# Row loads ahead of the small copies, two weight pieces shared between GpSimd and VectorE, and a new order around the group borders

## The reference

```python
q, k = rope(x @ Wq.T), rope(x @ Wk.T)            # bf16, one head of 256
o    = where(causal, exp(q @ k.T / 16), 0).sum(-1)   # one number per token
x1   = layernorm(x + relu(o * fc1_w + fc1_b) @ fc2_w.T + fc2_b)
xa   = x1 @ P_w.T                                # 64 values
C1, C2, C3 = top-3-of-12 softmax of xa @ U1.T, xa @ U2.T, xa @ U3.T
h    = gelu(sum_e C1[:, e] * (x1 @ W1[e].T))
y    = layernorm(x1 + sum_e C2[:, e] * (h @ W2[e].T) + C3 @ b2)
```

## Time and profile before

| | us |
|---|---|
| median of 3 runs | 297.56 |
| the profiled execution's own time | 297.77 |
| its span | 296.0 |
| busy TensorE / VectorE / GpSimd / ScalarE | 262.5 / 215.9 / 181.3 / 175.9 |

### The profile page before, as it was taken

How to read it: one execution, slowest core, us unless ns; L and a number is a source line. 1 busy time by engine, 2 the same in 40 slices (tenths; PEclk the granted TensorE clock), 3 DMA queues, 4 the chain that set the end, 5 groups by cost and what they waited for, 6 DMA issues and landing times.

```text
span 296.0 us, 6482 instructions
## 1 busy us (share of the span) xinstructions
PE 262.5 (89%) x2016; PEld 193.3 (65%) x2016; DVE 215.9 (73%) x668; ACT 175.9 (59%) x376; POOL 181.3 (61%) x367
## 2 busy tenths in 40 slices
PE   8999939999979597889799899898998998989960
PEld 5444414454536376767589798797897896878950
DVE  0369626969984965989599899899897877764660
ACT  2246932666565153655766967967878859464531
POOL 2630001897998999755676576785785765755532
PEclk9999995999999889999799999999999999999995
DMA  8997499998000000000000010101010010110101
GB/s 226 405 392 267 77 175 163 206 137 103 0 0 3 0 0 3 0 6 15 21 13 26 21 37 20 38 19 40 18 29 27 20 38 18 40 36 21 36 23 54
DMA packets 19546, 20.51 MB, mean 69 GB/s; under 512 B 1643, under 2 KB 18870, under 8 KB 18998
## 3 DMA queue, kind: packets, MB, share of 16 engines
q1 hardware_dynamic: 18518, 19.14, 28.2%
q10 hardware_dynamic: 992, 0.93, 1.1%
HBM read 15.78 MB, written 4.19 MB: 67 GB/s over the span
## 4 chain that ended last, share of the span: by engine, by line
PE 48%; POOL 15%; SPq 11%; DVE 11%; issue 6%; ACT 5%; DMA 2%; POOLq 0%; DVEq 0%; ACTq 0%
PE bank L1108 35%; PE bank L916 5%; POOL W L470 5%; POOL wtmp L467 4%; DVE early L1521 4%; POOL W L469 3%; SPq L393 2%; SPq L380 2%; DMA xs<-in_x 2%; PE bank L991 2%; SPq L371 2%; PE bank L1186 2%; SPq L398 2%; ACT early L726 1%; SPq L397 1%
## 5 line engine op out<-in xcount | busy, mean ns | idle before, releaser
L1108 PE MATMUL bank<-W,x1T 128*128 (+1 forms) x630 | 77.3, 278 | 6.0 <-DVE early L1521 3.1
L1108 PE MATMUL bank<-W,early 128*128 (+1 forms) x630 | 74.4, 273 | 3.0 <-DVE early L1561 1.3
L1108 PEld LDWEIGHTS bank<-W,x1T 128*128 128x128 f16 x630 | 61.7, 100 | 17.1 <-issue 5.5
L1108 PEld LDWEIGHTS bank<-W,early 128*128 128x128 f16 x630 | 61.0, 98 | 10.8 <-DVE early L1561 1.6
L916 PE MATMUL bank<-early,wqk 128*128 128x512 f32 x128 | 62.1, 617 | 0.2 <-DMA early<-in_xT 0.2
L1521 DVE SCALAR_TENSOR_TENSOR early<-bank,Csel,early 128x256 f32<-128x256 f32 x95 | 45.7, 481 | 15.7 <-PE bank L1108 6.7
L590 POOL TENSOR_TENSOR early<-early 128x256 f32<-128x256 f32 x29 | 21.1, 729 | 31.6 <-DVE early L1521 31.6
L661 ACT ACTIVATE qk<-bank 128x512 bf16<-128x512 f32 x32 | 19.0, 595 | 32.3 <-PE bank L916 32.2
L916 PEld LDWEIGHTS bank<-early,wqk 128*128 128x128 f32 x128 | 22.9, 195 | 21.0 <-issue 20.3
L787 ACT ACTIVATE early<-early 128x256 f32<-128x256 f32 x32 | 13.3, 417 | 36.5 <-DVE early L1521 36.4
L1274 DVE TENSOR_TENSOR xturn<-qk,turn 128x2048 bf16<-128x2048 bf16 x16 | 21.2, 1323 | 16.1 <-ACT qk L661 16.1
(11 more groups left out here) (139 smaller groups left out, 460.7 us busy)
## 6 DMA issues: line engine op xcount, KB each, us to landing
early<-in_xT SPq DMA_DIRECT2D x16, 256.0 KB, 8.5
xs<-in_x SPq DMA_DIRECT2D x32, 128.0 KB, 7.9
out<-early SPq DMA_DIRECT2D x32, 128.0 KB
W<-in_w1T SPq DMA_DIRECT2D x1, 2048.0 KB, 12.2
W<-in_w2T SPq DMA_DIRECT2D x1, 2048.0 KB, 12.9
W<-in_w1T SPq DMA_DIRECT2D x1, 1024.0 KB, 7.6
W<-in_w2T SPq DMA_DIRECT2D x1, 1024.0 KB, 14.6
wqk<-in_wqkT ACTq DMA_DIRECT2D x1, 512.0 KB, 3.7
```

Of the source, the lines that this page charges most:

```text
L1108: mm = pe.matmul(where[:, 0:DIM], lhs(hx, c), w, start=(k == 0), stop=(k == 5))
```

## The change

Six things change.

1. SyncE issues `load_rows(0)`, chunks 4 and 5 and `load_rows(1)` before the twelve copies.
2. Of the last two pieces of W2 (numbers 14 and 15; `SHARED` is 14) GpSimd makes only the high half, in one multiply from `Wf` to `W`. VectorE makes the low half (`piece_rest`). Piece 15 may only be written when VectorE has read piece 14's source.
3. GpSimd does `chosen_exps(0)` and `weights_of(0)` one piece earlier, and `bias_add(0, 0)` between the last two pieces.
4. TensorE's `route_count(0)` comes behind the third projection of chunk 7. Tile 0's second mixture takes the experts in the order 0 to 11, with other waits.
5. At the borders of groups 1, 6 and 7 TensorE does the first mixture of the group's first tile between the two bias halves; ScalarE's `final(1)` moves behind a `bias_copy`.
6. At the end VectorE does the statistics of tile 30 before the second mixture of tile 31.

```diff
@@ sync
-            sp.wait_ge(fc2_split, 1)
-            sp.wait_ge(b2_split, 1)
-            for k in range(NP):
-                sp.dma_start(fc2s[NI * k:NI * (k + 1), :], fc2p[:, RIGHT[k], :]).then_inc(fc2_spread, 16)
-                sp.dma_start(b2s[NE * k:NE * (k + 1), :], b2p[:, RIGHT[k], :]).then_inc(b2_spread, 16)
             load_rows(0)
             for c in range(4, NCH):
                 load_chunk(c)
                 if c % 2:
                     load_rows(c // 2 - 1)
+                if c == 5:
+                    sp.wait_ge(fc2_split, 1)
+                    sp.wait_ge(b2_split, 1)
+                    for k in range(NP):
+                        sp.dma_start(fc2s[...], fc2p[:, RIGHT[k], :]).then_inc(fc2_spread, 16)
+                        sp.dma_start(b2s[...], b2p[:, RIGHT[k], :]).then_inc(b2_spread, 16)
@@ gpsimd, w_piece (SHARED = NM * (NE - NB) - 2)
+                if n >= SHARED:
+                    if n == SHARED:
+                        pool.wait_ge(w_split, SHARED)
+                    else:
+                        pool.wait_ge(piece_low, n - SHARED)
+                    pool.tensor_scalar(W[:, m, e + 1, 0, :], Wf[:, WS * m + e + 2, :], scale[:, 1 + m:2 + m], 0.0,
+                                       ALU.mult, ALU.add).then_inc(piece_high, 1)
+                    return
@@ gpsimd
-                    if (c, j) == (6, 2):
+                    if (c, j) == (6, 1):
                         chosen_exps(0)
                         weights_of(0)
...
+            bias_add(0, 0)
             w_piece(piece)
...
-            bias_add(0, 0)
             norm_scale(2)
@@ scalar, aux
                 if (k, s, pos) == (1, 0, 0):
                     normed(3, 0)
-                    final(1)
                 if (s, pos) == (0, 1):
                     if group(k):
                         bias_copy(k, 0)
+                    if k == 1:
+                        final(1)
@@ tensor
+            def between(k):
+                return k in (1, NG - 2, NG - 1)
...
                     if group(k):
                         bias(k, 0)
+                    if between(k):
+                        routed_first(GT * k)
                     if later(k + 2):
                         x1_transpose(k + 2, 0)
...
+                if c == NCH - 1:
+                    route_count(0)
                 if c:
                     scores(c - 1, 1)
...
             route_logits(1)
+            pe.wait_ge(wlo_done, NM * NB)
+            second(0, range(0, NB))
             pe.wait_ge(w_split, NM * (NE - NB) - 2)
-            second(0, range(0, 6))
+            second(0, range(NB, NB + 2))
             bias(0, 1)
+            second(0, range(NB + 2, NE - 2))
             x1_transpose(2, 0)
-            pe.wait_ge(w_split, NM * (NE - NB))
-            second(0, range(6, NE - NB))
-            pe.wait_ge(wlo_done, NM * NB)
-            second(0, range(NE - NB, NE))
+            pe.wait_ge(piece_low, 2)
+            second(0, range(NE - 2, NE))
@@ vector
+            def piece_rest(n):
+                e = NB + n % (NE - NB)
+                dve.wait_ge(piece_high, n - SHARED + 1)
+                dve.scalar_tensor_tensor(W[:, 1, e + 1, 1, :], Wf[:, WS + e + 2, :], scale[:, 2:3], W[:, 1, e + 1, 0, :],
+                                         ALU.mult, ALU.subtract).then_inc(piece_low, 1)
...
             first_mixture(0, range(8, NE))
+            piece_rest(SHARED)
             norm_stats(2)
             h_low(0)
+            piece_rest(SHARED + 1)
             first_mixture(1)
...
                 aux(k, s, 0)
+                if i == NT + 1:
+                    row_stats(i - 3)
                 second_mixture(i - 2)
-                if late(i - 3):
+                if late(i - 3) and i <= NT:
                     row_stats(i - 3)
```

More of the change, by code:

```diff
@@ L199, in build @@
         KEPT = 10
+        SHARED = NM * (NE - NB) - 2
         ld_qk = sem("ld_qk")
@@ L232, in build @@
         wlo_done = sem("wlo_done")
+        piece_high = sem("piece_high")
+        piece_low = sem("piece_low")
         proj_done = sem("proj_done")
@@ L327, in build @@
         before = [max((k for k in range(n) if place[k] == place[n]), default=None) for n in range(len(taker))]
-        def dense_expert(m, j):
-            return (j + NB * m) % NE
         def last(t, m):
@@ L403, in _ @@
                     load_rows(c // 2 - 1)
+                if c == 5:
+                    sp.wait_ge(fc2_split, 1)
+                    sp.wait_ge(b2_split, 1)
+                    for k in range(NP):
+                        sp.dma_start(fc2s[NI * k:NI * (k + 1), :], fc2p[:, RIGHT[k], :]).then_inc(fc2_spread, 16)
+                        sp.dma_start(b2s[NE * k:NE * (k + 1), :], b2p[:, RIGHT[k], :]).then_inc(b2_spread, 16)
             load_rows(TPS - 1)
@@ L1069, in early @@
                     fc(k + 3, 0)
-                if (s, pos) == (3, 1) and group(k + 1):
-                    route_count(k + 1)
             def aux(k, s, pos):
@@ L1117, in mixture @@
                         pe.wait_ge(acc_begun if act else slot_added, count)
-                    e = dense_expert(m, j) + 1 if t == 0 else held_ids[t // GT][REC * m + j]
+                    e = j + 1 if t == 0 else held_ids[t // GT][REC * m + j]
                     products(bank[place[n]], lhs, m, e).then_inc(slot_done, 1)
@@ L1203, in _ @@
             route_logits(1)
+            pe.wait_ge(wlo_done, NM * NB)
+            second(0, range(0, NB))
             pe.wait_ge(w_split, NM * (NE - NB) - 2)
-            second(0, range(0, 6))
+            second(0, range(NB, NB + 2))
             bias(0, 1)
+            second(0, range(NB + 2, NE - 2))
             x1_transpose(2, 0)
-            pe.wait_ge(w_split, NM * (NE - NB))
-            second(0, range(6, NE - NB))
-            pe.wait_ge(wlo_done, NM * NB)
-            second(0, range(NE - NB, NE))
+            pe.wait_ge(piece_low, 2)
+            second(0, range(NE - 2, NE))
             h_transpose(1)
             routed_first(2)
+            fc(3, 0)
             route_count(1)
-            fc(3, 0)
             gate_transpose(2)
@@ L1230, in _ @@
                 aux(k, s, 1)
-                if i < NT:
+                if i < NT and (s or not between(k)):
                     routed_first(i)
@@ L1517, in add_slot @@
                 n = slot[t, m, j]
-                e = dense_expert(m, j) + 1
+                e = j + 1
                 c = C[:, 0, m, e:e + 1] if t == 0 else Csel[:, t, m, j:j + 1]
```

## The result

The changed kernel takes 286.70 us (median of 4 runs, 285.99 to 287.30) against 297.78 us for the kernel before (4 runs beside it): 0.9626 of the time, 95% interval 0.9587 to 0.9664. Run again later, beside a median of 298.49 us for the kernel before, the same program took 288.98 us (288.37 to 290.79), ratio 0.9700 [0.9658, 0.9742]. The profiled execution after took 285.99 us; its span is 284.2, the mean granted clock of TensorE in it 0.991 against 0.966.

A forecast was written before the change was run, and what follows sets the result against it. Bounds: TensorE's early stall with its slow clock, then GpSimd's end, then group borders and tail. 4.9 + 2.1 + 1.6 + 1.35 = 9.95 us off 297.77 gives 287.8, as median 287.6 (8 in 10: 283.8 to 292).

The forecast's parts named there:

- The stall and the slow clock behind it: TensorE's 5.00 us stall at 38.4 us and the half clock after it go: TensorE 8.1 us earlier, `scale` at about 47.
- The copies: Twelve small copies, some behind row block 1: the last lands and GpSimd starts at 50.0 (47 to 54), 4.1 us earlier.
- the second rival: All copies stand behind row block 1 and take 3.2 us; GpSimd starts at 51.2, time 288.8 us; chance 0.12.
- copies early: Copies do not hold GpSimd up: it starts at 47, 3 us less, time 284.7 us; chance 0.16.
- copies late: Copies let GpSimd start only at 54, as before; only the other terms are left, 291.6 us; chance 0.16.
- packet pace: Copy pieces as slow as row packets, about 13.8 us on one engine: GpSimd starts at 61.9, time 299.5 us; chance 0.04.
- the rival of a loaded VectorE: VectorE, busy from 118 to 141 us, loses two more microseconds and group 1 gains nothing: 291 us; chance 0.05.
- GpSimd up to the last gather: GpSimd's 1.53 us wait at 73.59 goes too: 5.6 us earlier from there, last gather ends at 105.5.
- The shared pieces: W2's last two pieces: VectorE waits 3.4 us, yet tile 0's second mixture begins at 111.1, 6.5 us earlier.
- The clock: Half clock behind TensorE's 3.9 us stand from 105.4 costs 1.6 us (0 to 2.2); 4.9 us gained at 126.14.
- Group 1: Border round of group 1: TensorE no longer waits for ScalarE's copies, 2.1 us less (0 to 4).
- Groups 6 and 7, tail: Borders of groups 6 and 7 give 1.6 us together (0 to 2.7); the tail up to the last `final` 1.35.

The follow-up runs named there:

- after_again: The changed kernel, unaltered, run once more: 288.98 us, 0.9700 of the kernel before.
- borders_back: The changed kernel with TensorE's old order at the borders of groups 1, 6 and 7, ScalarE's `final(1)` still moved: 289.73 us, 0.9697.
- pieces_whole: The changed kernel with GpSimd making pieces 14 and 15 whole, the bias add still between them: 285.44 us, 0.9577.
- bias_late: The changed kernel with GpSimd making pieces 14 and 15 whole and the bias add behind piece 15: 289.34 us, 0.9683.
- border1_old: The changed kernel with TensorE's old order at group 1's border and `final(1)` back ahead of the bias copy: 289.96 us, 0.9719.
- tail_back: The changed kernel with tile 30's statistics back behind the second mixture of tile 31: 289.39 us, 0.9711.
- border1_back: The changed kernel with TensorE's old order at the border of group 1 alone: 288.31 us, 0.9637.
- copies_mid: The changed kernel with the twelve copies between chunk 5 and row block 1: 287.44 us, 0.9606.
- exps_back: The changed kernel with group 0's exponentials one piece later on GpSimd, as before the change: 288.71 us, 0.9667.
- loads_only: The kernel before with the new order of the loads and nothing else: 291.15 us, 0.9744.

## Why the prediction was right, and where not

Predicted were 287.6 us (283.8 to 292.0) and faster; 286.7 and 289.0 were measured, eight executions from 285.99 to 290.79.

**The stall and the slow clock behind it.** Right. Block 0 let the add start at 36.49 (35.7 predicted), TensorE has no gap, `scale` is done at 47.0 (47).

**The copies.** The start came within the stated 2 us (48.90 for 50.0), but the step was wrong in how it gets there. The six fc2s copies share one semaphore, and the trace has its twelve steps up: six about 1.1 us behind the issues, which I take as posted at the issue, and six others, which I take as the landings (us):

| run | last rows of block 1 land | fc2s copies land | last one issued | GpSimd starts |
|---|---|---|---|---|
| after | 46.44 | 46.75, 47.13, 47.54, 47.97, 48.41, 48.81 | 46.81 | 48.90 |
| after_again | 47.40 | 47.73, 48.10, 48.52, 48.95, 49.39, 49.79 | 47.64 | 49.89 |
| borders_back | 45.36 | 45.69, 46.07, 46.47, 46.91, 47.31, 48.42 | 46.45 | 48.52 |

In the profiled execution the first copy, issued at 39.51, landed only at 46.75, 0.3 us behind the block, and the others followed 0.4 us apart; no packet of a copy's size (512 bytes) moved from 40.0 to 44.0, while three of them were issued. In all ten traces with that order the first landing is 0.3 to 0.4 us behind the block (GpSimd starts at 48.5 to 50.2). So every fc2s copy stood behind block 1: that is the second rival's mechanism, to which the prediction gave 0.12, and not "some copies". Its 51.2 did not come because the block landed at 46.4 and not at 48.0 and the six copies took 2.4 us and not 3.2. The issue of the last copy is a second bound, since no copy landed less than about 2.0 us after its issue: in borders_back and pieces_whole it is the later one, in the profiled execution the two fall together. The DMA engines show the same, busy with the block and then nearly idle:

```profile
39.50:44.00 4.50, 4.50 (x22) 2.44 (x21) 4.26 (x13) 2.21 (x6) 0.00 (x0) 1.00 1.15 160
46.50:49.00 2.50, 2.50 (x14) 1.38 (x13) 2.29 (x10) 2.38 (x8) 1.04 (x4) 1.00 0.08 22
```

That 50.0 was near is two errors against each other: the block was put 1.6 us too late, and the start 2.0 us behind it where it was 2.5. Rivals copies early, copies late, packet pace and the stall stays fell by the same rows. Two side sums of the rivals do not come out: by the prediction's own numbers gain turns to loss at a start of 60.0, not 60.8 (50.0 + 297.56 - 287.6), and the rival of a loaded VectorE gives 291.7, not 291 (287.6 + 2 + 2.1).

**GpSimd up to the last gather.** 7.8 us earlier in the profiled execution, 6.8 in the next, 5.6 predicted. Of the 2.2 us between 5.6 and 7.8, 1.1 is the start; 0.9 more came because the first five pieces took 17.1 us instead of 18.0, which the step had set equal.

**The shared pieces.** The start at 109.6 (111.1 predicted) hides that the step was credited with a gain that it does not have. The prediction saw VectorE's wait (3.4 us; it was 4.9, in other traces down to 3.1) and that the split of h stands behind it, but not that whole pieces would have let that split run at 104.2. It also named no wait ahead of the bias add; it waited for ScalarE's copy, 2.02 us here and 0.78 in five of the other traces with shared pieces. The gain belongs to the bias add between the pieces (2.7 us, bias_late), and the sharing costs 1.5 us at S0 at equal clock (pieces_whole).

**The clock.** The term of 1.6 us, within bounds of 0 and 2.2, was about right for the two traces of the changed kernel and wrong as a fixed place. G is 14.6 where no half clock falls between the last gather and S0 (border1_old, tail_back); it is 15.4 to 15.6 in four traces with a stretch of 3.4 us there (after, borders_back, border1_back, copies_mid), so 0.8 to 1.0 us, and 16.6 in after_again with one of 6.9 us, so 2.0. Over these seven traces the mean is 0.8 (exps_back, with its longer stall ahead of this stage, is left out). In the profiled execution the stretch lay ahead of the second mixture, in the next on it. This step makes 1.0 of the 2.0 us by which the two traces differ at S0; the other 1.0 is GpSimd's later start.

**Behind S0.** No term of the sum had a loss here, and 0.84 to 1.03 us are lost from S0 to S1 at full clock. The traces show a chain for it. `x1_transpose(2, 0)` now stands behind ten of tile 0's twelve products and not behind six, so ScalarE's copy of its result, the table load and two normalisations come later and run into its copy of tile 1's h; VectorE's split of h waits for that, its adds come 0.9 us later after S0, and TensorE's second `fc` of that place waits longer. Before, and then after:

```profile
130.27 1.10 PE L991 MATMUL bank<-fc2w,hgf 32*128 32x256 f32 x4 [0.29 <-DVE xs L1344]
```
```profile
119.19 0.45 ACT L839 ACTIVATE early<-bank,ipow 128x256 f16<-128x256 f32 x1
119.67 0.48 DVE L1584 SCALAR_TENSOR_TENSOR early<-bank,ipow,early 128x256 f16<-128x256 f32 x1 [0.88 <-ACT early L839]
123.12 1.10 PE L1001 MATMUL bank<-fc2w,hgf 32*128 32x256 f32 x4 [1.20 <-DVE xs L1367]
```

The wait is 1.19 or 1.20 us in all twelve traces with the new order of TensorE around tile 0, and 0.29 or 0.30 in before and loads_only. The change also swaps `fc(3, 0)` and `route_count(1)` at this place, which its list leaves out. No run undoes either, so this cause is read from traces and not shown by an experiment.

**Group 1.** The step failed as put: "it no longer waits for ScalarE's copies" gives 0.2 us, not 2.1. The rest of the 1.73 us measured between S1 and S2, 1.5, is the half clock behind the wait, which the prediction had read in the 3.66 of the earlier trace rows and not priced by itself.

**Groups 6 and 7, tail.** Right in kind: 1.1 us (tiles 21 to 29) where 1.6 were predicted, and 1.18 for 1.35 up to the last `final`. Another 0.5 us behind the last `final` was in no term.

**The sum** then reads, for the two traces of the changed kernel: S0 7.99 and 5.98 earlier (4.9 predicted), 0.84 and 1.03 lost from S0 to S1, 1.73 and 1.74 won from S1 to S2, 1.1 at groups 6 and 7, 1.7 in the tail with what follows it; 11.7 and 9.5 us in all, where the spans are 11.8 and 9.4 shorter and 9.95 was predicted. That the time came out near is in part luck: too small a gain ahead of S0 stood beside a border gain for the wrong reason and a loss behind S0 that no term had.

## What to carry to other kernels

Move small DMAs behind the loads that someone waits for, and count three things of them: the issue time (0.59 and 0.74 us each here), the loads ahead of them in the queue (here no fc2s copy landed before them), and the landing of the last (2.0 us after its issue at the least). Before two engines share the last of a job, look at what stands in the helper's queue behind the wait: here the split of h stood there, and undoing the sharing gave 1.5 us at equal clock. Price a TensorE wait twice, as a wait and as a half clock that may follow it or not and may fall here or there (0.8 to 2.0 us in the stage before S0), and compare order edits of 1 us between marks in traces, not by medians.

## What the runs showed of the hardware that was not expected

- The same stall of TensorE, about 2 us between 98.6 and 101, was followed by half clock in one trace and not in another with the same instructions up to there. S0 to S1 took 9.2 to 9.4 us in the three traces of new orders without a half-clock stretch in it, and 10.1 to 12.1 in the ten with one.
- GpSimd's instructions of one form have steps: the 128x512 cast mostly 0.61, 0.94 or 1.48 us, the multiply 0.69 to 2.18. Over all fourteen traces, each of the 83 casts of 0.94 us or more overlaps a rotation or weight instruction of VectorE, and 121 of the 123 of 0.61 overlap none.
- GpSimd's multiply straight to float16 takes 0.69 us, as that to float32.
- The issue of like DMAs does not take SyncE the same time: four chunk DMAs took 6.53 us at 27.8, behind loads that had not landed, and 2.16 at 48.2. That the unfinished loads hold the issue up is the likely reading; no run here shows it.
- The fc2s copies landed from 0.3 us after the last load ahead of them on and 0.4 us apart, though the first had been issued 7 us before (46.75 for 39.51).
